# Probabilities of one head in four turned on VectorE and assembled through device memory, instead of on TensorE

## The reference, cut to what matters

```python
q, k, v = (proj(Wq), proj(Wk), proj(Wv))
scores = jnp.einsum('bhsd,bhtd->bhst', q, k) * scale
scores = jnp.where(mask[None, None, :, :], -jnp.inf, scores)
attn = jax.nn.softmax(scores, axis=-1)
out = jnp.einsum('bhst,bhtd->bhsd', attn, v)
out = out.transpose(0, 2, 1, 3).reshape(B, S, E) @ Wo.T
xn = out / rms * rms_scale * (1.0 + sc[:, None, :]) + shift[:, None, :]
x = x + xn
```

## Time and profile before

| | us |
|---|---|
| median of 3 runs | 858.3 |
| profiled execution, first to last instruction | 855.4 |
| outside the span, against the median | 2.9 |
| PE busy | 846.5 (99%) |
| DVE busy | 628.7 (73%) |
| ACT busy | 615.9 (72%) |
| POOL busy | 482.5 (56%) |

### The profile page before, as it was taken

How to read it: one execution, slowest core, us unless ns; L and a number is a source line. 1 busy time by engine, 2 the same in 40 slices (tenths; PEclk the granted TensorE clock), 3 DMA queues, 4 the chain that set the end, 5 groups by cost and what they waited for, 6 DMA issues and landing times.

```text
span 855.4 us, 17179 instructions
## 1 busy us (share of the span) xinstructions
PE 846.5 (99%) x5344; PEld 640.8 (75%) x5344; DVE 628.7 (73%) x1524; ACT 615.9 (72%) x1504; POOL 482.5 (56%) x346
## 2 busy tenths in 40 slices
PE   9999999999999999999999999999999999999997
PEld 6788888888887777767777677776777767777774
DVE  5521321322338899999999999999999999999886
ACT  6232332232329899999999999999999999999882
POOL 0999990000000111666777667776677766777794
PEclk9999999999999999999999999999999999999999
DMA  8854644654599658786687775788668777569201
GB/s 288 339 212 164 233 172 184 220 185 183 182 284 272 138 112 231 173 203 147 149 204 162 157 207 135 156 185 209 143 148 204 164 160 207 131 157 245 68 26 51
DMA packets 82355, 153.76 MB, mean 180 GB/s; under 512 B 8520, under 2 KB 9160, under 8 KB 82272
## 3 DMA queue, kind: packets, MB, share of 16 engines
q1 hardware_dynamic: 82128, 152.49, 65.8%
q10 hardware_dynamic: 144, 0.26, 0.1%
HBM read 102.35 MB, written 50.36 MB: 179 GB/s over the span
## 4 chain that ended last, share of the span: by engine, by line
PE 97%; DVE 1%; issue 1%; ACT 1%; POOL 0%; DVEq 0%; ACTq 0%
PE banks L788 26%; PE banks L120 14%; PE banks L816 13%; PE banks L851 10%; PE banks L471 9%; PE banks L473 9%; PE banks L472 9%; PE banks L797 2%; PE banks L831 1%; PE banks L456 1%; PE banks L444 0%; DVE probs L685 0%; ACT turned_probs L1013 0%; PE banks L510 0%; DVE banks L955 0%
## 5 line engine op out<-in xcount | busy, mean ns | idle before, releaser
L137 ACT ACTIVATE probs<-probs,least 128x512 f32<-128x512 f32 x512 | 363.4, 713 | 0.0
L129 DVE CUSTOM_DVE_ANT_0 probs<-banks,mask_bias 128x512 f32<-128x512 f32 x512 | 330.0, 681 | 37.5 <-PE banks L120 37.5
L788 PE MATMUL banks<-ident,probs 128*128 128x128 f32 x2048 | 306.4, 272 | 0.8 <-DVE turned_probs L901 0.7
L788 PEld LDWEIGHTS banks<-ident,probs 128*128 128x128 f32 x2048 | 252.6, 140 | 56.7 <-ACT probs L137 2.0
L120 PE MATMUL banks<-k_rows,q_rows 128*128 128x512 f32 x496 | 236.2, 478 | 0.0
L901 DVE COPY turned_probs<-banks 128x512 f32<-128x512 f32 x256 | 175.5, 686 | 2.3 <-PE banks L788 2.3
L400 DVE SCALAR_TENSOR_TENSOR late<-banks,late 128x512 fp32r<-128x512 f32 x64 | 43.9, 690 | 158.7 <-ACT late L337 158.7
L1013 ACT ACTIVATE turned_probs<-banks 128x512 f32<-128x512 f32 x256 | 147.1, 587 | 17.0 <-PE banks L788 13.5
L685 POOL TENSOR_TENSOR late<-rot,late 128x2048 f32<-128x2048 f32 x28 | 129.2, 4615 | 0.0
L337 ACT ACTIVATE late<-banks 128x512 fp32r<-128x512 f32 x64 | 38.2, 598 | 119.6 <-PE banks L473 112.5
L816 PE MATMUL banks<-turned_probs,v_sb 128*32 128x512 f32 (+1 forms) x1088 | 117.0, 570 | 1.3 <-ACT turned_probs L1013 1.3
(11 more groups left out here) (134 smaller groups left out, 1263.0 us busy)
## 6 DMA issues: line engine op xcount, KB each, us to landing
q_rows<-q_scratch SPq DMA_DIRECT2D x128, 256.0 KB, 6.1
k_rows<-k_scratch SPq DMA_DIRECT2D x124, 256.0 KB, 6.5
q_scratch<-late SPq DMA_DIRECT2D x64, 256.0 KB, 2.3
k_scratch<-late SPq DMA_DIRECT2D x64, 256.0 KB, 2.3
v_sb<-v_scratch SPq DMA_DIRECT2D x8, 1024.0 KB, 11.4
out<-late SPq DMA_DIRECT2D x29, 256.0 KB, 7.5
raw<-in_xT SPq DMA_DIRECT2D x7, 1024.0 KB, 5.4
v_scratch<-v_out SPq DMA_DIRECT2D x28, 256.0 KB, 2.0
```

Of the source, the lines that this page charges most:

```text
L129: dve.tensor_tensor_reduce(self.probs[:, n % RING, :], self.ps[:, n % SCORE_BANKS, :], self.mask_bias[:, c, :], 1.0, 3e38, ALU.add, ALU.mi ...
L137: act.activation(self.probs[:, n % RING, :], self.probs[:, n % RING, :], ACT.Exp, bias=self.least[:, n % 32:n % 32 + 1], scale=-1.0, accum ...
L788: last = pe.transpose(turn_bank("tile", n)[:, j * P:(j + 1) * P], probs[:, n % RING, j * P:(j + 1) * P], ident[:, :])
```

## The change: what it does

In whole groups, the four tiles of the group's first head (places 0 to 3) are no longer turned on PE. DVE transposes each tile in its sixty-four 32x32 blocks from `probs` into a new buffer `blocks` (`block`, one instruction at each of t = 0 to 3). That puts 32 keys on 32 partitions for each quarter of the queries. SP then puts the quarters together (`move_blocks`): four stores of 256 KB, each from 32 consecutive partitions, to device memory, and, each after its store has landed, four loads of 256 KB to 128 partitions of `turned_probs`. The value product of that head waits for the loads and reads and writes its columns in pieces of 32.

The other twelve tiles are copied out eight by ACT and four by DVE ('----101101101101', where 1 is ACT), in place of eight and eight. MASKS, EXPS and the places of all else stay. q and k are loaded to every fourth partition instead of to 32 consecutive ones. To make room, the ring has 10 tiles instead of 12, and `scaled` and `junk` now lie in `o_T`, with waits added for that.

```diff
 N = U * TILES
-RING, SLOTS = 12, HG + 1
+RING, SLOTS = 10, HG + 1
...
-ORDER = [(v, u, i, c) for v, (u, chunks) in enumerate(GROUPS) for i in range(HG) for c in chunks]
+BLOCK_PLACES = (0, 1, 2, 3)
+BLOCKS_AT = (0, 1, 2, 3)
+def tiles_of_group(chunks):
+    tiles = [(i, c) for i in range(HG) for c in chunks]
+    if chunks == ALL:
+        blocked, tiles = tiles[:TC], tiles[TC:]
+        for place, tile in zip(BLOCK_PLACES, blocked):
+            tiles.insert(place, tile)
+    return tiles
+ORDER = [(v, u, i, c) for v, (u, chunks) in enumerate(GROUPS) for i, c in tiles_of_group(chunks)]
...
-BY_ACT = {'early': '0101010101010101', 'whole': '0101010101010101', 'half': '01010011'}
+BY_ACT = {'early': '----101101101101', 'whole': '----101101101101', 'half': '01010011'}
+TURNS = [n - BY_ACT[:n].count("-") for n in range(len(BY_ACT) + 1)]
...
-        sp.dma_start(f32(self.q[r * D:(r + 1) * D, u % 2]),
+        sp.dma_start(f32(self.q[r::HG, u % 2]),
                      self.scr["q"][u, r % 2].rearrange("(i d) t -> d i t", d=D)).then_inc(self.q_in[u % 2], 16)
     def load_k(self, sp, u, r):
-        sp.dma_start(f32(self.k_of(u)[r * D:(r + 1) * D]),
+        sp.dma_start(f32(self.k_of(u)[r::HG]),
...
-        if n >= RING:
-            dve.wait_ge(self.turned, n - RING + 1)
+        if n >= RING and BY_ACT[n - RING] == "-":
+            dve.wait_ge(self.blocked, n - RING + 1 - TURNS[n - RING + 1])
+        elif n >= RING:
+            dve.wait_ge(self.turned, TURNS[n - RING + 1])
...
+        def chunks_of(v):
+            return GROUPS[v][1]
...
+            def move_blocks(v):
+                sp.wait_ge(blocked, TC * (v + 1))
+                if v >= 2:
+                    sp.wait_ge(moved, 16 * TC * (v - 1))
+                for a in (0, 2, 1, 3):
+                    sp.dma_start(scr["blocks"][v % 2, a].rearrange("(k p) t -> p k t", p=D),
+                                 blocks[a * D:(a + 1) * D].rearrange("p k j c t -> p k (j c t)")).then_inc(blocks_out[a], 16)
+                if v >= 2:
+                    sp.wait_ge(valued, v - 1)
+                for a in (0, 2, 1, 3):
+                    sp.wait_ge(blocks_out[a], 16 * (v + 1))
+                    sp.dma_start(turned_probs[:, HG * v % SLOTS, a, :], scr["blocks"][v % 2, a]).then_inc(moved, 16)
...
                     store(v - NG - 2)
+                if chunks == ALL:
+                    move_blocks(v)
...
-                    last = pe.matmul(value_ps[i * D:(i + 1) * D, cols], v_sb[:, b % 2, part, h * D:(h + 1) * D],
-                                     turned_probs[:, (HG * u + i) % SLOTS, part, cols],
+                    to, of = value_ps[i * D:(i + 1) * D, cols], turned_probs[:, (HG * u + i) % SLOTS, part, cols]
+                    if i == 0 and chunks == ALL:
+                        if part == 0:
+                            pe.wait_ge(moved, 16 * TC * (v + 1))
+                        to = to.rearrange("p (c a t) -> p a c t", c=TC, a=TC)
+                        of = turned_probs[:, HG * u % SLOTS, :, part * P:(part + 1) * P].rearrange(
+                            "p a (c t) -> p a c t", c=TC)
+                    last = pe.matmul(to, v_sb[:, b % 2, part, h * D:(h + 1) * D], of,
...
-                turn(n)
+                if BY_ACT[n] != "-":
+                    turn(n)
...
+            def block(n):
+                v, u, i, c = ORDER[n]
+                dve.wait_ge(exped, n + 1)
+                if n == 0:
+                    dve.wait_ge(projected, (TC + 2 * NG) * (B - 1) + 2 * NG)
+                for a in range(TC) if c == 0 and v > 0 else ():
+                    dve.wait_ge(blocks_out[a], 16 * v)
+                dve.transpose(blocks[:, :, :, c, :].rearrange("p k j t -> p j k t"),
+                              probs[:, n % RING, :].rearrange("p (j k t) -> p j k t", j=TC, k=TC)).then_inc(blocked, 1)
             def move_out(n):
                 v, u, i, c = ORDER[n]
                 h = HG * u + i
-                dve.wait_ge(turned, n + 1)
+                dve.wait_ge(turned, TURNS[n + 1])
...
+                if NG <= v < POOL_GROUPS:
+                    dve.wait_ge(summed, v - NG + 1)
...
                 dve.wait_ge(squared, m + 1)
+                dve.wait_ge(o_ready, min(m + NG, POOL_GROUPS))
...
-                dve.wait_ge(turned, N)
+                dve.wait_ge(turned, TURNS[N])
...
+                if chunks_of(v) == ALL and t in BLOCKS_AT:
+                    block(FIRST[v] + BLOCK_PLACES[BLOCKS_AT.index(t)])
```

More of the change, by code:

```diff
@@ L105, in __init__ @@
         self.least = ctx.enter_context(nc.sbuf_tensor("least", [P, 32], F32))
-        self.scored, self.masked, self.exped, self.turned, self.inverted, self.spread, self.passed = [
+        self.scored, self.masked, self.exped, self.turned, self.blocked, self.inverted, self.spread, self.passed = [
             ctx.enter_context(nc.semaphore(n))
-            for n in ("scored", "masked", "exped", "turned", "inverted", "spread", "passed")]
+            for n in ("scored", "masked", "exped", "turned", "blocked", "inverted", "spread", "passed")]
     def score(self, pe, n):
@@ L184, in projections @@
         square = setup[:, 12 * C:24 * C].rearrange("p (q d) -> p q d", d=C)
[L185 to L188, removed]
+        term = setup[:, 12 * C:28 * C].rearrange("p (j i d) -> p j i d", j=4, i=4)
+        gate_b = setup[:, 28 * C:29 * C]
+        mask_words = setup[:, 29 * C:33 * C].bitcast(mybir.dt.int32).rearrange("p (c t) -> p c t", c=TC)
+        mask_u8 = setup[:, 29 * C:33 * C].bitcast(U8).rearrange("p (c t) -> p c t", c=TC)
         row_least = sb("row_least", [P, TC], F32)
@@ L596, in attention @@
         probs, den = scores.probs, scores.den
-        scored, masked, exped, turned = scores.scored, scores.masked, scores.exped, scores.turned
+        scored, masked, exped, turned, blocked = scores.scored, scores.masked, scores.exped, scores.turned, scores.blocked
         inverted, spread, passed = scores.inverted, scores.spread, scores.passed
@@ L603, in attention @@
         turned_probs = sb("turned_probs", [P, SLOTS, TC, S])
+        blocks = sb("blocks", [P, TC, TC, TC, D])
         inv = sb("inv", [P, HG, TC])
@@ L609, in attention @@
         x_s = late[:, 4:6, :]
-        scaled = sb("scaled", [P, E])
-        junk = sb("junk", [P, E], BF16)
+        scaled, junk = o_T, o_T[:, 0:E // 2].bitcast(BF16)
         sum_sq = sb("sum_sq", [P, 2])
@@ L617, in attention @@
         neg_half = sb("minus_half", [P, 1])
-        mix = late[:, 0:4, :]
+        mix, held_v = late[:, 0:4, :], late[:, 0, :]
         acc = late[:, 6:8, :]
@@ L631, in attention @@
         valued, normed = sem("valued"), sem("normed")
+        blocks_out = [sem(f"blocks_out{a}") for a in range(TC)]
+        moved = sem("moved")
         o_hi_ready, o_ready = sem("o_hi_ready"), sem("o_ready")
@@ L647, in attention @@
                 PLACES.append(("scale", v - 1))
-            PLACES.append(("tile", n))
+            if BY_ACT[n] != "-":
+                PLACES.append(("tile", n))
         PLACES.append(("scale", V - 1))
@@ L689, in attention @@
         rows.last_k = values_and_k[:, 0]
-        late_mix = [probs[:, 4 * j:4 * j + 4, :] for j in range(3)]
+        late_mix = [probs[:, 4 * j:4 * j + 4, :] for j in range(2)] + [blocks[:, :, :, :, :].rearrange(
+            "p k j c t -> p k (j c t)")]
+        late_junk = probs[:, RING - 1, 0:E // 2].bitcast(BF16)
         late_out = [turned_probs[:, 3, j, :] for j in range(3)]
@@ L783, in turn @@
                 pe.wait_ge(exped, n + 1)
-                if n < 2:
-                    pe.wait_ge(qk_lo_ready, 2 * NG * B - 2 + n)
+                if PLACE["tile", n] < 2:
+                    pe.wait_ge(qk_lo_ready, 2 * NG * B - 2 + PLACE["tile", n])
                 bank_free(pe, "tile", n)
@@ L923, in held_out @@
                     dve.wait_ge(held_stored, 16 * c)
-                dve.tensor_copy(scaled[:, :], y_ps).then_inc(held_copied, 1)
+                else:
+                    dve.wait_ge(qk_stored[0], 16 * 4 * B)
+                dve.tensor_copy(held_v, y_ps).then_inc(held_copied, 1)
             def rescale(m):
@@ L984, in _ @@
                     split_lo(v - 1)
-                if not by_act(n - 1) and n > 0:
+                if n > 0 and BY_ACT[n - 1] == "0":
                     move_out(n - 1)
@@ L1009, in move_out @@
                 h = HG * u + i
-                act.wait_ge(turned, n + 1)
+                act.wait_ge(turned, TURNS[n + 1])
                 if h >= SLOTS:
@@ L1051, in late_square @@
                     act.wait_ge(late_squared, j)
[L1052 removed]
+                act.activation(late_junk, y_of(LATE[j]), ACT.Square,
                                accum_out=late_sum_sq[:, j:j + 1]).then_inc(late_squared, 1)
@@ L1072, in _ @@
                     split_hi(v - 1)
-                if by_act(n - 1) and n > 0:
+                if n > 0 and by_act(n - 1):
                     move_out(n - 1)
```

7 lines of the change are left out of this document (5 added, 2 removed).

## The result

The changed kernel takes 899.3 us (median of 4 runs, 897.9 to 901.9) where the kernel before, on the same chip, takes 858.25 (857.25 to 858.86): ratio 1.048, 95% interval 1.047 to 1.050. It is 4.8% slower; 894.0 was forecast. The profiled span is 897.9 us against 855.4, so 42.5 us are to be found.

What follows compares the result with a forecast made beforehand. PE set the pace, with DVE and ACT right behind; after the change ACT closes the loop. 26 periods x 1.30 plus 3 x 0.62 gave 35.7 us, so 858.3 + 35.7 = 894.0 us; range 872 to 930.

Steps and rivals of the forecast that it cites:

- PE's freed time doesn't arrive: Whole groups: three turns less on PE (1.05 us) shorten nothing; ACT closes the loop, period 17.82 to 19.12 us.
- The walk's stations: Start and end times in one whole group, followed from the value products' start V to ACT's last copy at V + 18.43.
- T = 0.60: Time of one block transpose on DVE, taken as 0.60 us, between bounds of 0.34 and 1.21.
- rival 3: Block transpose on DVE takes 1.21 us; mask 9 comes 1.22 later, period 20.34, 929 us; 12 in 100.
- ACT has its work without a gap: From copy 6 at V + 9.90, exponentials, six copies and the square follow unbroken to the last copy at V + 18.43.
- Early periods: First three of the 29 periods, which hold no square: +0.62 us each.
- Round trip hidden: Blocks' last load lands at V + 12 to 20.2, needed at 19.12: hidden over most of that, 1.1 us late at the end.
- Half groups and the projections hardly change, 0 within 1 us each: Parts of the kernel outside whole groups: no change, within 1 us each.
- The clock in the periods: PE busy some 16.4 of 19.1 us (86%) keeps its granted clock at the upper level: nothing.
- the shared `o_T`: Added waits are for work a group old or earlier in DVE's list: nothing; at most 2 us a group if uncovered.
- the ring: Ring of 10 tiles binds nowhere: masks 14 and 20 need turns 4 and 10, each four places back.
- the 32-column pieces: First head's value product in pieces of 32 columns: taken as nothing, at most +0.9 us a group.

Runs made afterwards that it cites:

- the two misses with seven copies: ACT makes seven copies a group instead of eight: 901.1 us in the changed kernel, 865.6 us with its four transposes also moved ahead of tile 8's mask.
- seven copies, first run: The changed kernel with seven copies on ACT instead of eight ('----101010101011'): 901.1 us, ratio 1.050 to the kernel before.

## Why the prediction was right, and where it was off

- **PE's freed time doesn't arrive, and a loop over DVE's masks and ACT's copies closes at 19.1 us: right.** 19.04 measured. The walk's stations came out at V + 4.68 and 7.09 (masks 8 and 9, exactly), 7.81 (exponential 9, exactly), 6.86 (copy 4, 6.82 said), 9.94 (copy 6, 9.90 said) and 18.39 (last copy, 18.43 said). ACT's waits are 0.84, 0.60, 0.35 and 0.61 where 0.84, 0.65, 0.51 and 0.67 were said.
- **What holds ACT is the mask behind the transposes: right**, and shown by moving them.
- **T = 0.60: right**, 1.23 us for two (511.48 to 512.71). The price of a slow transpose (rival 3, 58 us for each us of T) is right at the full clock: 0.74 of added T cost 43 us in the periods. It left out the clock: in all, the doubled transposes cost 66 us (965.2 - 899.3), 22 of them in the 13 periods in which it fell.
- **"ACT has its work without a gap" to the end: right for the time, wrong as an account of what it is worth.** The turn of tile 10 starts at 519.10 and is only just ready for its copy, 0.64 later, so there is a second path to that copy, through PE, as long as ACT's own. The prediction said of tiles 7, 9 and 10 that they are ready before their copies, but not by how little; the two misses with seven copies follow from that.
- **Early periods: 0.46 us too small each.** 315.79 - 296.89 = 18.90 where 18.44 follow from the sum. Without the square the last copy waits 0.33 us for the turn of tile 15, which itself waits for a bank. Times 3, 1.4 us. The 26 others are 19.05 on the mean, 0.07 shorter than 19.12, as the square takes 0.57 (524.01 to 524.58) where 0.68 were taken. That the two errors cancel is luck: 35.4 for 35.7.
- **Round trip hidden: right in the periods.** By SP's timeline the last load's issue ends at 519.22; by the median of 3.6 us it lands at V + 16.6, between the ends given (12 and 20.2), 2.4 us ahead of need. Not counted was the first group, whose wait of 2.02 us is most of the 3.6 lost at the start; without the round trip 2.3 of them go.
- **"Half groups and the projections hardly change, 0 within 1 us each": the step that failed**, by 3.5 us at the end. SP's list had been read for who waits in a whole group, but not for what the eight new DMAs of a group push back where the groups run out. They take SP 6.4 us (512.81 to 519.22, with its waits for the stores' landing). In the tail the load of x that POOL needs is issued 1.3 us later against the value products and takes 1.6 longer to arrive.
- The clock in the periods, the shared `o_T`, the ring and the 32-column pieces at nothing: right. The value products take 3.64 us as before.

Together: 35.4 + 3.6 + 3.5 = 42.5 against a forecast of 35.7. The kernel's time rose by 41.0 (899.3 - 858.25), since it stands 1.4 above its span where 2.9 were taken. So the miss of 5.3 us is the 7.1 at the two ends, made smaller by 1.5 and by 0.3 in the periods. The 1.5 is luck: in every other execution of the kernel before, its time stands 1.7 to 1.9 above its own span, so the profiled one was some 1 us quicker than the median it was set beside.

## What to carry to other kernels

In this kernel, where three engines hand tiles around, taking work off the one that was full gave nothing until the order on the others was rewritten. Follow one period from its latest fixed event, and put added work into the idle time ahead of that event, not behind it. A copy or a transpose has no price of its own; a copy taken off ACT was worth 0 or 13 us by standing ahead of or behind the turn that ACT waits for. Count the first and the last period apart, since what is hidden by earlier work is bare in the first, and a longer issue list is paid in the last.

## What had not been expected of the hardware

- **TensorE's granted clock after a short rest.** With each transpose twice, a rest of 2.5 us is followed by a clock of 0.50 for some 3 us in 13 groups, and by 1.00 in 16. The first group's value products show the same in other runs. With the transposes early they wait 2.91 us and take 5.34 us instead of 3.64:

```profile
277.71 5.34 PE L864 MATMUL banks<-turned_probs,v_sb 128*32 128x512 f32 x32 [2.91 <-DMA turned_probs<-blocks_scratch]
```

  They take 5.34 behind a wait of 2.49 us too (seven copies, first run), but 3.64 behind 2.71 (seven copies, one fewer behind the turn of tile 10) and behind 2.02 (the changed kernel). So the length of the rest alone doesn't say whether the clock falls. The changed kernel's tail has a gap of 3.15 us, and behind it the clock is 0.66 from 863 to 866:

```profile
863.00:866.00 3.00, 2.77 (x12) 2.21 (x13) 3.00 (x10) 1.68 (x4) 3.00 (x2) 0.66 0.01 3
```

- **Loads onto every fourth partition take SP longer to issue.** An issue of q_rows took 0.43 us before (median, 300 to 800 us) and takes 0.60 in the changed kernel. The fuller queue is not the reason: it is 0.60 as well in the runs with everything but the blocks and without the round trip, which have no DMA more than the kernel before.
- **The way through device memory is quick.** The blocks' stores land 3.9 us after issue and their loads 3.6 (medians), each 256 KB, with the DMA share at 0.84. The stores, from 32 consecutive partitions, are thus hardly slower than the loads onto 128. At that share the loads of q still land in 4.6 us, sooner than the 6.1 of before.
